# Four transformer layers on one core: query rows by way of an expanded buffer, and turned maxima and sums taken by ScalarE

## The reference

```python
x = L0(x, ctx)   # windowed self-attention, 16 heads of 64, windows of 64 keys + 32 extra keys; gated feed-forward
x = L1(x, ctx)   # cross-attention to ctx (6404 rows), 16 heads of 8, softmax; feed-forward with gelu
x = L2(x, ctx)   # cross-attention to ctx, 16 heads of 8, softmax; layer norm
x = L3(x, ctx)   # layer norm, masked self-attention; layer norm, cross-attention to ctx; layer norm, feed-forward
# each cross-attention, for head h:
Q = (q_in @ wq + bq)[h] / sqrt(8); K = (ctx @ wk + bk)[h]; V = (ctx @ wv + bv)[h]
out[h] = softmax(Q @ K.T) @ V
```

## Time and profile before

| | |
|---|---|
| median of 3 runs | 4291.36 us (4289.76 to 4299.0) |
| profiled execution | 4295.77 us, span 4294.0 us |
| mean granted clock of TensorE | 0.906 |
| TensorE busy | 3623.7 us, 84% of the span |
| VectorE busy | 3432.7 us, 80% |
| ScalarE busy | 2790.2 us, 65% |
| GpSimd busy | 230.6 us, 5% |
| DMA | 114.79 MB, mean 27 GB/s |

### The profile page before, as it was taken

One profiled execution on the slowest core, in us unless ns is written; L12 is line 12 of the kernel. 1 busy time (PEld: TensorE's weight loads), 2 busy tenths in 40 slices (PEclk: granted clock), 3 DMA queues, 4 the chain that ended last, 5 costly groups with the idle time before them and its releaser, 6 DMA issues. The chain is left out here.

```text
span 4294.0 us, 85387 instructions
## 1 busy us (share of the span) xinstructions
PE 3623.7 (84%) x35064; PEld 1221.9 (28%) x35126; DVE 3432.7 (80%) x3358; ACT 2790.2 (65%) x3989; POOL 230.6 (5%) x196
## 2 busy tenths in 40 slices
PE   5675799999999927999999997289848999999995
PEld 2352322222222212222222222045422222222221
DVE  4322799999999618999999995389949999999972
ACT  0431288888888813888888886145515888888884
POOL 3000000000000000000000000234400000000000
PEclk9657599999999966999999999599958999999998
DMA  3102011111110140111111102300011011101100
GB/s 99 47 1 45 13 22 19 27 27 21 21 27 15 48 61 12 27 19 22 27 27 21 20 15 59 71 11 6 3 22 25 15 27 27 27 14 27 27 4 21
DMA packets 56293, 114.79 MB, mean 27 GB/s; under 512 B 10594, under 2 KB 46306, under 8 KB 50946
## 3 DMA queue, kind: packets, MB, share of 16 engines
q1 hardware_dynamic: 55940, 109.79, 14.4%
HBM read 84.16 MB, written 25.50 MB: 26 GB/s over the span
## 5 line engine op out<-in xcount | busy, mean ns | idle before, releaser
L1727 DVE TENSOR_REDUCE chunk_max<-max_scores 128x2 f32<-128x988 f32 (+1 forms) x2496 | 2790.7, 1179 | 157.4 <-PE max_scores L1597 122.0
L1708 ACT ACTIVATE probs<-scores 128x512 f32<-128x512 f32 (+1 forms) x3231 | 2452.9, 808 | 550.0 <-PE scores L1623 527.3
L1650 PE MATMUL values_sum<-probs,values 128*9 128x256 f32 x19584 | 1376.2, 383 | 26.7 <-DVE values_sum_s L1738 18.5
L1623 PE MATMUL scores<-queries,key_ring 49*128 49x512 bf16 x4800 | 1230.9, 385 | 44.5 <-ACT probs L1708 11.8
L1597 PE MATMUL max_scores<-key_ring,queries 48*128 48x494 bf16 (+1 forms) x4992 | 982.1, 391 | 130.0 <-DVE chunk_max L1727 114.4
L1650 PEld LDWEIGHTS values_sum<-probs,values 128*9 128x9 f32 x19584 | 376.9, 89 | 794.0 <-issue 572.4
L1623 PEld LDWEIGHTS scores<-queries,key_ring 49*128 49x128 bf16 x4800 | 305.8, 94 | 640.3 <-ACT probs L1708 537.0
L1597 PEld LDWEIGHTS max_scores<-key_ring,queries 48*128 48x128 bf16 x4992 | 241.0, 94 | 821.9 <-DVE chunk_max L1727 543.3
L1317 ACT ACTIVATE probs<-scores 128x512 f32<-128x512 f32 x256 | 138.0, 590 | 105.3 <-PE scores L1269 105.3
L1689 ACT ACTIVATE values<-scores 128x512 f32<-128x512 f32 (+2 forms) x45 | 25.1, 565 | 239.8 <-PE scores L1607 227.0
L1343 DVE TENSOR_REDUCE chunk_max<-max_scores 128x1024 f32 (+1 forms) x128 | 155.0, 1214 | 26.8 <-PE max_scores L1225 26.6
(11 more groups left out here) (190 smaller groups left out, 1713.1 us busy)
## 6 DMA issues: line engine op xcount, KB each, us to landing
key_ring<-k_parts SPq DMA_DIRECT2D x96, 300.2 KB
key_ring<-k_parts SPq DMA_DIRECT2D x96, 200.1 KB
key_ring<-k_parts SPq DMA_DIRECT2D x96, 100.1 KB
k_parts<-queries SPq DMA_DIRECT2D x72, 128.0 KB, 2.4
o_whole<-values_sum_s SPq DMA_DIRECT2D x48, 128.0 KB, 7.3
k_parts<-k_part SPq DMA_DIRECT2D x36, 128.0 KB, 2.4
queries<-q_parts SPq DMA_DIRECT2D x36, 128.0 KB
context<-in_ctx_t SPq DMA_DIRECT2D x1, 3202.0 KB, 17.2
```

Source lines behind the costliest of these rows:

```text
L1623: return pe.matmul(sc[:, g % 3, :], keys(rows, h, P * t, P * (t + 1)), qb[rows, q], start=True, stop=True)
L1650: mm = pe.matmul(acc[32 * b:32 * b + WV, 0:QBLOCK], vb[rows, h, t, :], pr[rows, slot, QBLOCK * (b % 2):QBLOCK * (b % 2 + 1)], start=(t == ...
L1708: act.activation(pr[:, a % RING:a % RING + b - a, :], sc[:, a % 3:a % 3 + b - a, :], ACT.Exp)\
L1727: dve.tensor_reduce(mx[:, h % 2, c, :, j], mxb[:, w % 2, :, 0:width], AX.X, ALU.max)\
```

## The change

- Windowed attention: TensorE computes the scores in two halves, one before `values(s - 2, 0)` and one before `values(s - 2, 1)`; VectorE copies pair s - 3's outputs before it masks pair s; ScalarE copies what was turned one step earlier in its own order, behind the exponentials.
- Query terms of the cross-attentions: the parts are stored six-fold, in the order of the rows (`q_rows`, half, 48 rows, head, query), with six DMAs from SP and six from ScalarE's queue. Then SP reads two rectangles of 48 partitions for heads 0 and 1, which the block waits for, and two for the other 14 heads, which TensorE waits for at the first unit of head 2. The self-attention's query terms are stored as before.
- Cross-attention: ScalarE casts the turned maxima (`turn`), for heads 1 to 15 behind the exponential of the op after the one in which they are turned, and copies the sums (`take_values`) before the exponential of the op after the one with the head's last tile. The turn has semaphores of its own. VectorE keeps the reductions and the next key terms, which it starts when the last reduction is done.
- Opening: TensorE no longer waits for the cleared accumulator, and one value projection follows the second of each four units, 13 times; none runs ahead.

```diff
         def _(pe):                                    # windowed_attention
-            def scores(p):
-                if p >= 1:
+            def scores(p, c):
+                if p >= 1 and c == 0:
                     pe.wait_ge(masked_ready, 2 * p)
-                for t in range(QT):
+                for t in range(4 * c, 4 * (c + 1)):
...
                 if s < NPAIR:
-                    scores(s)
+                    scores(s, 0)
                 if s >= 2:
                     values(s - 2, 0)
                     turn(s - 2, 1)
+                if s < NPAIR:
+                    scores(s, 1)
+                if s >= 2:
                     values(s - 2, 1)
...
+                if s >= 3:
+                    pair_out(s - 3)
                 if s < NPAIR:
                     mask_and_maximum(s)
-                if s >= 3:
-                    pair_out(s - 3)
...
-            for s in range(NPAIR + 2):
-                if s >= 2:
-                    copies(s - 2, 0)
+            for s in range(NPAIR + 1):
                 if s < NPAIR:
                     exps(s, 0)
-                if s >= 2:
-                    copies(s - 2, 1)
+                if s >= 1:
+                    copies(s - 1, 0)
                 if s < NPAIR:
                     exps(s, 1)
+                if s >= 1:
+                    copies(s - 1, 1)
...
+            if q_rows is not None:                    # query_terms, ScalarE
+                for p, ready in enumerate((high, middle, low)):
+                    act.wait_ge(ready, 2)
+                    store_query_rows(act, q_rows, part, p, 1, stored)
...
+                store_query_rows(sp, q_rows, part, p, 0, stored)
+            sp.wait_ge(stored, 16 * (NPART if q_rows is None else 2 * NTERM))
+            if q_rows is not None:
+                for half in range(2):
+                    load_query_rows(sp, rows_of, q_rows, half, 0, 2).then_inc(fetched, 16)
+                for half in range(2):
+                    load_query_rows(sp, rows_of, q_rows, half, 2, H).then_inc(rest_fetched, 16)
+                sp.wait_ge(fetched, 32)
+
+def store_query_rows(engine, q_rows, part, p, half, stored):
+    for r in range(K_RUNS[p]):
+        row = FIRST_ROW[p] + HD * r
+        engine.dma_start(q_rows[half, row:row + HD].rearrange("d h n -> h d n"), cols(part[p], half))\
+              .then_inc(stored, 16)
+
+def load_query_rows(sp, rows_of, q_rows, half, lo, hi):
+    return sp.dma_start(rows_of[64 * half:64 * half + KROWS, HALF * lo:HALF * hi],
+                        q_rows[half, :, lo:hi].rearrange("r h n -> r (h n)"))
...
             def max_step(w):                          # cross_attention, TensorE
-                if w >= 2:
-                    pe.wait_ge(max_taken, w - 1)
+                if w >= 2 and max_entry(w - 2)[1] is None:
+                    pe.wait_ge(turn_taken, max_entry(w - 2)[0] + 1)
+                elif w >= 2:
+                    pe.wait_ge(max_taken, units_before(w - 1))
...
-            pe.wait_ge(acc_zeroed, 1)
-            for c in range(3):
-                value_projection(c)
             for u in range(HEAD_UNITS + LEAD):
                 max_step(u)
-                if u % 4 == 3 and u // 4 + 3 < NCHUNK:
-                    value_projection(u // 4 + 3)
+                if u % 4 == 1 and u // 4 < NCHUNK:
+                    value_projection(u // 4)
+            pe.wait_ge(acc_zeroed, 1)
...
+            def take_values(h):                       # ScalarE
+                act.wait_ge(tile_used, NTILE * (h + 1))
+                if h >= 2:
+                    act.wait_ge(o_stored[h % 2], 16 * (h // 2))
+                act.activation(acc_s[:, h % 2, :], acc[:, 0:QBLOCK], ACT.Copy).then_inc(acc_taken, 1)
+            def turn(h):
+                w = turn_entry(h)
+                act.wait_ge(turn_ready, h + 1)
+                if h >= 1:
+                    act.wait_ge(rows_loaded, 32 * h)
+                act.activation(nrow[:], mxb[0:QT, w % 2, 0, 0:P], ACT.Copy).then_inc(turn_taken, 1)
+            turn(0)
+            turn_after = {turn_op(h) + 1: h for h in range(1, H)}
             for n in range(NOPS):
+                if n >= 1 and tiles_by[n - 1] % NTILE == 0 and tiles_by[n - 1] > (tiles_by[n - 2] if n >= 2 else 0):
+                    take_values(tiles_by[n - 1] // NTILE - 1)
...
+                if n in turn_after:
+                    turn(turn_after[n])
```

More of the change, by code:

```diff
@@ L96, in __init__ @@
         self.steps = 0
+        self.rest_rows = [ctx.enter_context(nc.semaphore(f"rest_rows_{n}")) for n in range(3)]
         self.first_keys = [ctx.enter_context(nc.semaphore(f"first_keys_{n}")) for n in range(3)]
@@ L691, in scores @@
                                        start=True, stop=True)
-                mm.then_inc(scores_ready, 1)
+                if c == 1:
+                    mm.then_inc(scores_ready, 1)
             def turn(p, c):
@@ L911, in query_terms @@
         low = sem("low")
-        stored = [sem("stored") for _ in range(NPART)]
+        stored = sem("stored")
         fetched = sem("fetched")
@@ L949, in _ @@
                 sp.wait_ge(ready, 2)
[L950 to L960, removed]
-                sp.wait_ge(fetched, 16 * 2 * NTERM)
+                if q_rows is None:
+                    sp.dma_start(q_parts[:, p], part[p][:]).then_inc(stored, 16)
+                    continue
+                store_query_rows(sp, q_rows, part, p, 0, stored)
[14 more added lines that the diff above has]
+                        q_rows[half, :, lo:hi].rearrange("r h n -> r (h n)"))
 def key_value_terms(k, src, tk, ni, wk, bk, wv, bv_row, k_parts, vb, qb, q_parts,
@@ L1472, in max_entry, with units_before, turn_op @@
     return h, (v if v < TURN_AFTER else v - 1)
+def units_before(w):
+    return w - sum(turn_entry(h) < w for h in range(H))
+def turn_op(h):
+    return next(n for n in range(NOPS) if entries_through(n) > turn_entry(h))
 def turn_entry(h):
@@ L1519, in cross_attention @@
         max_taken = sem("max_taken")
+        turn_ready = sem("turn_ready")
+        turn_taken = sem("turn_taken")
         head_max = sem("head_max")
@@ L1546, in max_rows @@
             def max_rows(h):
-                sp.wait_ge(max_taken, turn_entry(h) + 1)
+                sp.wait_ge(turn_taken, h + 1)
                 for half in range(2):
@@ L1593, in max_step @@
                 elif u == 0:
+                    if h == 2:
+                        pe.wait_ge(k.rest_rows[layer], 32)
                     pe.wait_ge(keys_loaded[h % KRING], 16 * 2 * NPART * (h // KRING + (1 if h % KRING == 2 else 0)))
@@ L1658, in next_key_product @@
                 if c == 0:
-                    pe.wait_ge(max_taken, NENTRY)
+                    pe.wait_ge(max_taken, H * HEAD_UNITS)
+                    pe.wait_ge(turn_taken, H)
                 if c >= 4:
@@ L1709, in _ @@
                    .then_inc(exp_ready, 1)
+                if n in turn_after:
+                    turn(turn_after[n])
+            for h in range(tiles_by[NOPS - 2] // NTILE, H):
+                take_values(h)
         @block.gpsimd
@@ L1718, in take_entry @@
                 h, u = max_entry(w)
-                dve.wait_ge(max_scores, w + 1)
                 if u is None:
-                    if h >= 1:
-                        dve.wait_ge(rows_loaded, 32 * h)
-                    dve.tensor_copy(nrow[:], mxb[0:QT, w % 2, 0, 0:P]).then_inc(max_taken, 1)
                     return
+                taken = units_before(w)
+                dve.wait_ge(max_scores, taken + 1)
                 c, j = u // 4, u % 4
@@ L1765, in _ @@
             dve.memset(acc[:], 0.0).then_inc(acc_zeroed, 1)
-            dve.wait_ge(acc_zeroed, 1)
-            w = 0
-            for h in range(H):
-                if h == H - 1 and ahead is not None:
-                    for c in range(NCHUNK):
-                        next_key_terms(c)
-                last = next((n for n in range(NOPS) if tiles_by[n] >= NTILE * (h + 1)), NOPS - 1)
-                while w < entries_through(last):
-                    take_entry(w)
-                    w += 1
-                take_values(h)
+            for w in range(NENTRY):
+                take_entry(w)
+            if ahead is not None:
+                for c in range(NCHUNK):
+                    next_key_terms(c)
 def cross_output(k, o_whole, bv, out_t):
```

15 lines of the change are left out of this document (6 added, 9 removed).

## The result

The changed kernel takes 4193.28 us (median of 4 runs, 4189.05 to 4196.85), the one before 4290.56 us beside it (4 runs, 4285.91 to 4299.0): a ratio of 0.9771, with a 95% interval of 0.9753 to 0.9789. That is 97 us faster; the forecast was 4201 us, in a range of 4160 to 4243. The profiled execution took 4189.05 us, with a span of 4186.9 us, where before it was 4295.8 and 4294.0. These two differ by 107 us, since the execution traced before stands 4 us over its median and the one traced after 4 us under it.

The account below looks back on a forecast made before the run. It took VectorE's chunk maxima and the score-to-exponential loop to bound the heads, with nobody working between head loops. Gains 52.5 + 6 + 5 + 16 + 11 = 90.5 us off 4295.8 gave 4205.3, median forecast 4201 us, range 4160 to 4243.

Parts of the forecast that it names:

- Part 1: Query rows between head loops: faster stores and reads cut VectorE's idle time before three memsets to some 10.2 us, gaining 52.5.
- Part 2: Openings of the cross attentions: maxima start about 0.6 us after entry, gaining 6 us in all, bounds 0 and 15.
- Part 3: Windowed attention: earlier output copies shorten a pair from 22.24 to 20.7 us, gaining 5 us, bounds -2 and 9.
- Part 4: Cross-attention heads: casts and copies move from VectorE to ScalarE, gaining 16 us, plus 11 from TensorE's vanished stop.
- the relief: Cross-attention heads: VectorE rid of casts and copies, net of the late row, 0.35 us a head over 45 heads, 16 us.
- the half clock: Head loops: TensorE's 1.06 us stop and nine following 3.4 us stretches at 1.2 GHz go, 9 x 1.25 = 11 us.
- The floor: Cross-attention heads: the loop from score to exponential and back, 3.51 us per six slots, takes 59.1 us a head.
- (a): Rival: head loops gain all that VectorE gives up, 1.22 x 45 = 55 us in place of 16; 4162 us, chance 0.13.
- (b): Rival: late row stops TensorE 1 us at every head and the half clock stays; 4253 us, chance 0.15.
- (d): Rival: slower than before, the late row stopping TensorE with half clock at each of 45 heads; 4332 us, chance 0.04.
- (c): Rival: query-row stores are as slow as the old reads, so 52.5 us of gain goes; 4253 us, chance 0.09.
- (e): Rival: ScalarE copies do not share Exp's table, two loads for each of 96 moved operations, +246; 4474 us, chance 0.02.

Follow-up runs that it names:

- a1: Changed kernel with the query rows written and read as before (three stores, then twelve reads, all waited for): 4247.56 us, ratio 0.9892 to the kernel before.
- a2: Changed kernel with the windowed attention's order of scores, copies and output pairs as before: 4190.24 us, ratio 0.9766 to the kernel before.
- a3: Changed kernel with the old opening, TensorE waiting for zeroed sums and making three value projections ahead: 4200.76 us, ratio 0.9787 to the kernel before.
- a4: Changed kernel with the cast of turned maxima and the copy of sums back on VectorE, key terms placed as before: 4231.96 us, ratio 0.9857.
- c1: Changed kernel with all twelve query-row stores issued by SP, none by ScalarE: 4199.06 us, ratio 0.9773 to the kernel before.
- d1: Changed kernel with both the cast of turned maxima back on VectorE and the windowed attention's old order: 4183.06 us, ratio 0.9743 to the kernel before.
- b1: Changed kernel with only the cast of turned maxima back on VectorE, the copy of sums left on ScalarE: 4185.22 us, ratio 0.9757.
- b3: Changed kernel with VectorE reducing only the first half of each unit's keys to maxima: 4015.01 us, ratio 0.9363 to the kernel before.
- c2: Changed kernel with the new stores, but rows read by twelve transfers of eight partitions, all heads, all waited for: 4260.91 us, ratio 0.9923.

## Why the prediction was right, step by step

The undone parts add up: a1 54.3, a2 -3.0, a3 7.5, a4 38.7 us, 97.4 in all against 97.3 for the whole change. That they agree so closely is luck, since each is uncertain by some 8 us and the ratios give 93 in all. Against the profiled execution the sum of 90.5 us was 16 short of 107; against the medians it was 7 short.

- **Part 1**, 52.5 us, was 56.5 in the trace and 54 by a1. The idle time was put at 10.2 us and is 8.9: from the low part (395.97) to the reads' issue (400.91) it took 4.9 us, where 5.2 had been reckoned, and from there to the memset 4.0, where it was 5.0. That the stores take their landing from the row of the key stores held: 2.3 to 3.0 us each at the first opening of the kernel after. These key stores were not alone on their queue, as the prediction has it; they start in threes 0.6 us apart and overlap, which made the row the better guide. The estimate of 11.4 us from the 138 GB/s of the Trainium skill, DMA: Bandwidth & Descriptors, "Bandwidth", does not hold here: the twelve stores took 7.0 us from their first issue (393.88) to the issue of the reads, and c1 shows that even one queue loses only 2.5 us.
- **Part 2**, 6 us, was 9.2 from memset to first nmax and 8.5 with the two stretches behind it; a3 says 6.6 by its trace and 7.5 by the medians, and leaves room for 2 to 8. The mechanism was right, the size inside its bounds of 0 to 15. Too small was the wait ahead of the first maxima: 5.76 us was taken for all three openings, and the other two had 6.67 and 6.49.
- **Part 3**, 5 us, is the part that the runs do not bear out. The pair is 20.52 us, against 20.7 forecast and 22.24 before, and the 4.6 us wait before TensorE's turns is there as 4.55 us. First score to low part took 227.3 instead of 236.6 us in this pair of traces: 2.8 of these 9.3 us are a clock that rises at 328.7 instead of some 345 us (in three of eleven kernels with the new order), and 6.5 the order. But a2 and d1 have the old order, and their times show no loss. The step took for granted that the clock stays at 0.50 all through the windowed part, as the trace of before shows it; with the old order it can rise twice and pay for 4.0 us. At a like clock behind the windowed part the new order is still 2.8 us ahead (230.1 against 227.3 us), which is too little for the times to show.
- **Part 4**, 16 us for the relief and 11 for the half clock, was 33.7. Nine stretches went, at 1.4 us (1.25 forecast) 12.8 of it; the other 21 are 0.5 us a head, where 0.35 had been taken. The split inside was wrong: I credited the relief to fewer entries on VectorE, hence to the cast as well as to the copy. b1 puts the 45 casts back on VectorE and the head gets shorter, 60.36 us. All of it is the copy, and that the 0.35 us reckoned came near the 0.5 measured was luck. The likely reason is TensorE's stop of 1.06 us at every third head, 0.35 us a head, which the prediction counted only with the half clock; the remaining 0.15 us are not traced to a cause. The row's wait of 0.4 us at every third head was right (4.17 instead of 3.83 us from turn to first score, 0.34), and to it came the maxima's buffer, which the prediction did not name.
- **The floor.** The 59.1 us, worked out from a cycle of 3.51 us for six slots, is not one: b3 runs at 58.05.
- **The rivals.** (a), the copy and entries' full 1.22 us a head, would with the half clock's end have cut 66 / 45 = 1.5 us from a period of 61.3 on average: 0.8 us came, a little over half. (b) and (d) needed a stop at each head; there is one at every third. (c) is refuted by the 8.95 us of idle time, (e) by the count of table loads.

## What to carry to other kernels

Look for what waits in series between the stages before you trim the loops: three idle stretches of 28 us gave more than half of the gain, and they show in no list of costly groups, only in the timeline and in windows with every engine at zero. When work is moved between engines, ask who waits for its result; the copy, for which TensorE stood, was worth 38 us, the cast, for which nobody stood on VectorE's side, was worth nothing or less, as it got later. And when a stage runs at half clock, a shorter pair in one trace is no proof of a shorter stage: undo that part alone.

## What I had not expected of the hardware

- In a2 and d1 TensorE's granted clock rises from 0.50 to 1.00 for 3.4 us twice within the windowed part; in the kernel before, with the same order, it stays at 0.50 in both places, and TensorE is busy for 3.40 of 3.40 us there in all three. The rises fell at the same two pairs in both traces, but with one trace of each kernel what decides it is left open.
- TensorE's clock alone moves the end of the first query block by 3 us among kernels that are alike up to there (227.1 to 230.3 us), and with it the comparison of any two single traces.
- VectorE, busy for 562.8 of 580 us in b1, takes a cast of 0.27 us a head without a longer head. At 97% it was still not what a head waited for at that place.
- Reads of DRAM into eight partitions moved 60 to 66 GB/s with a DMA share of 0.50 in each of the two layouts (a1, c2); the same bytes into 48 partitions took 18.7 - 8.95 = 9.7 us more than the first two heads alone.
